# Keys of the first attention spread over the heads by 8 DMAs a tile instead of by multiplies with a mask, with the projected rows in another order

## The chip, the cores and the metric

One core of one Trainium2 chip runs the kernel. The metric is the device time in microseconds (us) from the first to the last instruction with what lies around them: 362.15 us, the median of 3 runs (362.09 to 362.67). The engines are TensorE (PE), VectorE (DVE), ScalarE (ACT), GpSimd (POOL) and SyncE (SP), which here only issues DMAs.

## The reference

Two layers work on x of shape (16, 64, 256), each an attention and a feed-forward block with a layernorm ahead and x added behind. The change touches the first attention only: 8 heads of 8 dimensions over 256 positions, for each of 16 batch entries.

```python
qkv = x @ w_in.T + b_in                      # x is the transposed, normalised input
scores = jnp.einsum('bqhd,bkhd->bhqk', q, k) / sqrt(8)
scores = jnp.where(band, scores, neg)        # |query - key| <= 64
attn = jax.nn.softmax(scores, axis=-1)
o = jnp.einsum('bhqk,bkhd->bqhd', attn, v)
y = relu(o @ w_out.T + b_out) * encodings
out = jnp.einsum('nit,io->not', y, w_ct) + b_ct
```

The feed-forward block of layer 0 picks the upper half of the tokens by a score and works on these; layer 1 has an attention of 32 heads and a squared-relu block with a mixture term.

## The kernel before

x stands in SBUF as 8 tiles of 128 rows; a tile holds two batch entries (b = 0, 1). The first attention runs as a software pipeline written by hand. Every engine walks the same list of slots `(T_, l)`, 16 slots a tile, and in each slot issues what its own `slot_` function says for it; the order within an engine is fixed by that code, and semaphores tie the engines together. `(T_, l)` works on unit `16 * T_ + l` of the scores, and on other steps with a lag.

A unit is one (b, g, c, w): batch entry, group of four heads, half of the queries, pair of heads. Its steps are

- the scores matmul into bank `S` (L339): the queries of a group are the weights, the keys of two heads the 384 moving columns;
- on DVE the band mask and the row maximum (L1110), two custom instructions for a unit;
- after 8 units four transposes of the maxima (L349), which ACT writes into rows 96 to 127 of `qp` (L791);
- 11 slots behind, two transposed score matmuls into `ST` (L361), then exp on ACT (L785), the band on POOL by four affine selects for two units (L978 to L985), and 16 slots behind the product with v (L377).

One matmul gives all heads of a group apart because the keys are spread: `kb` holds for each head j of a group a copy of the projected keys `kp` in which all rows but those of head j are zero. In rows 96 to 99 it holds a one for head j, which takes the maximum off. `kp` and `qp` carry each value in three rows (`r` = 0 to 2) as parts of a split into a rounded and a remaining piece. In the kernel before, row `32 r + 8 j + d` is part r of dimension d of head j, so the 24 rows of a head stand in three runs of 8.

The spread copies of a tile are written by

- POOL, three times 128x1024: `keys` (L953 to L961), `kp` times `kmask`, for (b, g) = (0,0), (0,1), (1,0), in the slots of the table `KB`;
- ACT, four times 128x256: L753 to L763, for (b, g) = (1,1), in the slots of `KA`.

They are made one tile ahead, in the slots `T_ = t - 1`: slots 3, 6, 9 and 12 (`PROJ`) project keys of group 0, keys of group 1, queries of group 0 and of group 1. ACT writes `hs`, the rounded piece, from the bank (L751), and DVE mixes it into `kp` or `qp` a slot later (L1208, semaphore `dve_mix`). `kb` is double buffered: for tile t the copy waits for `pe_st` of tile t - 2.

The start: ACT's queue loads `w0`, `b0`, `kmask` and `wv0`; DVE rounds `w0` to `w0h` (L1084), multiplies `b0` into `sb0` (L1086), normalises tile 0 (L1077) and takes the remainder `w0l` (L1094), which the first projection needs. SP's queue loads x and, behind it, all other weights.

The second half (layer 0's feed-forward, then layer 1) starts in the last slots of the pipeline and is not changed.

Of the kernel before, what the change touches and what calls it, by code (L numbers as in the profile page):

```python
# [47 lines left out]
def build(nc, a):  # L48
    ctx = ExitStack()
    with ctx:  # L50
# [93 lines left out]
        names = ("ld_first ld_w0 ld_small ld_x1 ld_x ld_rest ld_late st_out "  # L144
# [106 lines left out]
        def _(sp):  # L251
# [19 lines left out]
            late = [(b1[:, :], a["b1"]),  # L271
# [10 lines left out]
            assert len(late) == 12  # L282
# [7 lines left out]
        LATE = 16 * 12  # L290
# [3 lines left out]
        def _(pe):  # L294
            mm, tr = nc.tensor.matmul, nc.tensor.transpose

            def project(t, n):

                if n == 0:
                    pe.wait_ge(s["act_xh"], t + 1)  # L300
                    pe.wait_ge(s["dve_xl"], t + 1)
                    if t == 0:
                        pe.wait_ge(s["dve_w"], 4)
                bank = proj_bank(t, n)
                if t >= 1:
# [8 lines left out]
            def values(t):
                if t >= 1:
                    pe.wait_ge(s["dve_mix"], 4 * t + 4)
                if t == 0:
                    pe.wait_ge(s["ld_small"], 64)
# [181 lines left out]
            for T_, l in SLOTS_ALL:  # L500
# [3 lines left out]
                if T_ == 1 and l == 10:  # L504
                    pe.wait_ge(s["dve_w"], 5)
# [199 lines left out]
        def _(act):  # L705
# [5 lines left out]
            load(b0[:, :], a["b0"], "ld_w0")  # L711
            load(kmask[:, :], a["kmask"], "ld_small")
            load(wv0[:, :], a["wv0"], "ld_small")

            def slot_(T_, l):

                t = T_ - 2
                if 0 <= t < TILES:
# [23 lines left out]
                if 0 <= t < TILES:  # L742
                    if l - 1 in PROJ:
# [3 lines left out]
                        if m == 0:  # L747
                            act.wait_ge(s["dve_w"], 4)
                        if m >= 2:
                            act.wait_ge(s["dve_mix"], m - 1)  # L750
                        A(r32(hs[:, m % 2, :]), proj_bank(t, n)[:, :], ACT.Identity, bias=sb0[:, n:n + 1], scale=cols[:, n // 2:n // 2 + 1])\  # L751
                            .then_inc(s["act_hs"], 1)
                for t, j in ((T_ + 1, KA.get(l)), (T_, KA.get(l + UNITS))):  # L753
                    if j is not None and 0 <= t < TILES:
                        if j == 0:
                            act.wait_ge(s["dve_mix"], 4 * t + 2)
                            if t == 0:
                                act.wait_ge(s["ld_small"], 64)
                            if t >= 2:
                                act.wait_ge(s["pe_st"], UNITS * (t - 1))  # L760
                        last = A(r32(kb[:, t % 2, 1, j, 1, :]), kp[:, 1, 1, :], ACT.Copy, scale=kmask[:, j:j + 1])
# [174 lines left out]
        def _(pool):  # L936
# [16 lines left out]
            def keys(t, b, g):  # L953

                pool.wait_ge(s["dve_mix"], 4 * t + g + 1)
                if t == 0 and (b, g) == (0, 0):
                    pool.wait_ge(s["ld_small"], 64)
                if t >= 2:
                    pool.wait_ge(s["pe_st"], UNITS * (t - 2) + 8 * b + 4 * g + 4)
                G.tensor_tensor(r32(kb[:, t % 2, g, :, b, :]), kp[:, g, b:b + 1, :].to_broadcast([P, 4, T]),  # L960
                                kmask[:, :, None].to_broadcast([P, 4, T]), ALU.mult).then_inc(s["pool_kb"], 1)  # L961

            def slot_(T_, l):
# [24 lines left out]
                if l in KB and 0 <= t < TILES:  # L988
# [78 lines left out]
        def _(dve):  # L1067
# [22 lines left out]
            dve.wait_ge(s["dve_w"], 2)  # L1090
            dve.wait_ge(s["dve_zero"], 1)
            for b in range(2):
                hp = slice(64 * b, 64 * b + 64)
                V.tensor_tensor(r32(w0l[hp, b, :, :]), w0[hp, :, :], w0h[hp, :, :], ALU.subtract).then_inc(s["dve_w"], 1)  # L1094

            def slot_(T_, l):
# [96 lines left out]
                if (T_, l) == (-1, 2):  # L1193
                    dve.wait_ge(s["ld_small"], 64)
# [264 lines left out]
```

## Time and profile before

| | |
|---|---|
| runs | 362.09, 362.15, 362.67 us |
| profiled execution | 362.1 us, span 360.4 us |
| PE busy | 320.2 us (89% of the span) |
| DVE busy | 256.2 us (71%) |
| ACT busy | 208.1 us (58%) |
| POOL busy | 192.7 us (53%) |
| chain that ended last | PE 58%, DVE 27%, issue 8%, ACT 3% |

The span is from the first to the last instruction of the profiled execution; its own time has 1.7 us more. Busy shares over the whole span mix stages: DVE is near full in the first attention (to about 170 us) and far from it later. So the rows below are taken by stretch. A tile of the pipeline takes about 21 us of it.

### The profile page before, as it was taken

To read this page: it belongs to the slowest core of one execution; us is meant where nothing else is said; L and a number is where in the kernel's file an instruction comes from. 1 tells how busy PE (TensorE), PEld (TensorE's weight loads), DVE (VectorE), ACT (ScalarE), POOL (GpSimd) and SP (SyncE) were. 2 spreads that over 40 slices of the span, in tenths; PEclk is the share of its full clock that TensorE was granted. 3 is DMA by queue.
4 is the path that set the end of the run, shared out by engine and by line. 5 is a ranking of instruction groups with operands and counts; after the bars stand their busy time and mean duration, and the time that the engine had idled before them with its cause. 6 is when DMAs were issued, how large, how long until landed. Compare 5 with 4: busy or idle time off the path is not lost.

```text
span 360.4 us, 7398 instructions
## 1 busy us (share of the span) xinstructions
PE 320.2 (89%) x2258; PEld 252.3 (70%) x2258; DVE 256.2 (71%) x935; ACT 208.1 (58%) x438; POOL 192.7 (53%) x287
## 2 busy tenths in 40 slices
PE   0689999779798898999999999899999999999993
PEld 0467768567576666767777777777777767888892
DVE  5899999999989899988323615576478846661364
ACT  2639888759687695967841341467577865213210
POOL 4757988758767585856602431515152543244733
PEclk9859999999999999999999999999999999999997
DMA  7996000000000000000000000000000000000011
GB/s 220 363 373 227 1 3 3 1 2 3 1 2 0 3 3 1 3 2 2 2 2 0 0 2 0 1 2 0 2 3 0 2 0 3 0 31 15 1 38 37
DMA packets 10150, 12.16 MB, mean 34 GB/s; under 512 B 1920, under 2 KB 8832, under 8 KB 10112
## 3 DMA queue, kind: packets, MB, share of 16 engines
q1 hardware_dynamic: 9536, 11.36, 9.2%
q8 instruction: 20, 0.33, 0.4%
q10 hardware_dynamic: 576, 0.33, 0.4%
q14 instruction: 18, 0.15, 0.1%
HBM read 10.64 MB, written 1.05 MB: 32 GB/s over the span
## 4 chain that ended last, share of the span: by engine, by line
PE 58%; DVE 27%; issue 8%; ACT 3%; POOL 2%; DMA 1%; POOLq 0%; DVEq 0%; SPq 0%; ACTq 0%
DVE masked L1110 10%; PE S L666 6%; PE S L339 5%; PE O L377 4%; PE ST L690 4%; PE S L472 4%; PE ST L361 4%; PE S L608 2%; PE S L536 2%; PE PJ L449 2%; PE PJ L579 2%; PE O L623 2%; PE PJ L310 2%; DVE st L1072 2%; PE XB L597 2%
## 5 line engine op out<-in xcount | busy, mean ns | idle before, releaser
L1110 DVE CUSTOM_DVE_ANT_0 masked<-S,band 128x192 bf16<-128x192 f32 x256 | 79.1, 353 | 8.4 <-PE S L339 7.3
L785 ACT ACTIVATE ex<-ST 128x384 f32<-128x384 f32 x128 | 62.2, 489 | 14.0 <-PE ST L361 13.4
L339 PE MATMUL S<-qk 128*128 128x384 f32 x128 | 53.5, 424 | 10.2 <-DVE mw L1110 8.1
L948 POOL TENSOR_SCALAR rstd<-mv 128x1 f32<-128x1 f32 x40 | 11.8, 294 | 94.2 <-DVE mv L1074 94.0
L960 POOL TENSOR_TENSOR qk<-kp,kmask 128x1024 fp32r<-128x1024 f32 x24 | 46.3, 1934 | 5.0 <-DVE kp L1208 4.9
L361 PE MATMUL ST<-qk 128*128 128x192 f32 x256 | 48.7, 273 | 0.0
L361 PEld LDWEIGHTS ST<-qk 128*128 128x128 f32 x256 | 44.5, 189 | 1.9 <-issue 1.2
L339 PEld LDWEIGHTS S<-qk 128*128 128x128 f32 x128 | 24.8, 195 | 23.3 <-issue 16.1
L1254 DVE TENSOR_REDUCE mw<-S 128x8 f32<-128x512 f32 x32 | 22.0, 687 | 17.9 <-PE S L536 17.8
L751 ACT ACTIVATE hs<-PJ,sb,cols 128x512 fp32r<-128x512 f32 x29 | 22.5, 777 | 20.6 <-PE PJ L311 20.1
L377 PE MATMUL O<-ex,v 128*32 128x192 f32 x512 | 34.2, 338 | 0.0
L690 PE MATMUL ST<-down,hT 128*128 128x256 f32 x128 | 28.9, 379 | 0.0
L310 PE MATMUL PJ<-xs,w0h 128*128 128x256 f32 x58 | 18.6, 340 | 11.1 <-DVE xs L1191 10.0
L978 POOL TENSOR_SCALAR_AFFINE_SELECT ex<-ex 128x256 f32<-128x256 f32 x32 | 14.3, 448 | 24.4 <-ACT ex L785 24.3
L983 POOL TENSOR_SCALAR_AFFINE_SELECT ex<-ex 128x512 f32<-128x512 f32 x32 | 20.6, 642 | 12.2 <-ACT ex L785 12.2
L690 PEld LDWEIGHTS ST<-down,hT 128*128 128x128 f32 x128 | 23.8, 190 | 2.9
L951 POOL TENSOR_TENSOR rstd<-rstd,cols 128x1 f32<-128x1 f32 x40 | 22.7, 569 | 3.3
L666 PE MATMUL S<-qk 128*128 128x512 f32 x96 | 24.3, 402 | 0.0
L310 PEld LDWEIGHTS PJ<-xs,w0h 128*128 128x128 f32 x58 | 12.0, 206 | 15.8 <-issue 15.3
L895 ACT ACTIVATE ex<-ST 128x512 f32<-128x512 f32 x32 | 19.1, 597 | 5.3 <-PE ST L549 4.9
L1008 POOL TENSOR_TENSOR qk<-kp,kmask 128x512 fp32r<-128x512 f32 x16 | 16.5, 1056 | 9.9 <-DVE kp L1223 5.6
L1110 DVE DVE_READ_ACCUMULATOR2_ANT mw<- 128x1 f32 x256 | 21.2, 83 | 0.0
(178 smaller groups left out, 757.9 us busy)
## 6 DMA issues: line engine op xcount, KB each, us to landing
w<-in_w SPq DMA_DIRECT2D x2, 1024.0 KB, 10.1
cx<-in_cx SPq DMA_DIRECT2D x1, 1024.0 KB, 7.9
cxT<-in_cxT SPq DMA_DIRECT2D x1, 1024.0 KB, 9.6
up<-in_up SPq DMA_DIRECT2D x1, 1024.0 KB, 10.9
down<-in_down SPq DMA_DIRECT2D x1, 1024.0 KB, 11.8
out<-x SPq DMA_DIRECT2D x8, 128.0 KB, 1.7
x<-in_x SPq DMA_DIRECT2D x1, 768.0 KB, 5.6
vecs<-in_vecs SPq DMA_DIRECT2D x1, 640.0 KB, 8.0
```

Source lines behind the costliest of these rows:

```text
L310: mm(bank[:, T * b:T * b + T], r32(w0h[:, n, :]), r32(xs[:, b, :]), start=True, stop=False)
L339: mm(out, r32(qp[:, t % 2, g, b, P * c:P * c + P]), r32(mv_), start=True, stop=True).then_inc(s["pe_s"], 1)
L361: last = mm(ST[n % 2][:, WIN * h:WIN * h + WIN], r32(kb[:, t % 2, g, 2 * w + h, b, P * c:P * c + P]), r32(qp[:, t % 2, g, b, BAND * c:BAND ...
L377: last = mm(O[32 * j:32 * j + 32, T * g + BAND * c:T * g + BAND * c + WIN], v0[:, t % 2, c, b, 4 * g + j, :], ex[:, (n // 2) % 4, j, :], s ...
L666: last = mm(S[m % 2][:, :].rearrange("p (t c) -> p t c", t=4), r32(up2[:, a, k, P * f:P * f + P]), r32(xq[half][:, :, b, k, :]), start=(i ...
L690: last = mm(ST[t % 2][:, 0:T], hT[:, f, P * m:P * m + P], down[:, f, :], start=(f == 0), stop=(f == FC - 1))
L751: A(r32(hs[:, m % 2, :]), proj_bank(t, n)[:, :], ACT.Identity, bias=sb0[:, n:n + 1], scale=cols[:, n // 2:n // 2 + 1])\
L785: A(ex[:, (n // 2) % 4, 2 * w:2 * w + 2, :], ST[n % 2][:, 0:2 * WIN].rearrange("p (h k) -> p h k", h=2), ACT.Exp, scale=SCALE).then_inc(s[ ...
L951: G.tensor_tensor(rstd[:, t:t + 1], rstd[:, t:t + 1], cols[:, 2:3], ALU.pow).then_inc(s[done], 1)
L960: G.tensor_tensor(r32(kb[:, t % 2, g, :, b, :]), kp[:, g, b:b + 1, :].to_broadcast([P, 4, T]), kmask[:, :, None].to_broadcast([P, 4, T]), ...
L1110: last = V.tensor_tensor_reduce(out=masked[:, n % 2, h, :], in0=S[n % 2][:, WIN * h:WIN * h + WIN], in1=band[:, c, :], scale=1.0, scalar=N ...
L1254: V.tensor_reduce(mw[:, k % 2, 2 * g:2 * g + 2, 96:100], S[0][:, :].rearrange("p (i j k) -> p i j k", i=2, j=4), AX, ALU.max).then_inc(s[" ...
```

## The change

- The rows of a head become neighbours: row `24 j + 8 r + d` instead of `32 r + 8 j + d`. The host hands over the same arrays as before. The columns of `w0` are put in the new order on the chip, by a copy on ACT that writes `w0h` rounded (in place of DVE's L1084) and a copy on POOL into `w0p`, a free part of `hT`. `b0` is loaded in five DMAs instead of one. The masks by part and by head (`part0`, `kmask0`) are made by DVE from `ident`, which now is loaded ahead of the band; `kmask` goes to the end of SP's small loads.
- For tiles 0 and 1 POOL and ACT write `kb` as before, with `kmask0`.
- From tile 2 on 8 DMAs a tile on SP's queue copy the 24 rows of each head from `kp` to its block of `kb`: four (one for each head of a group, both groups in one DMA) for b = 0, four for b = 1. The zeros and the rows 96 to 127 of both buffers stay as tiles 0 and 1 left them. The first four wait for both key mixes of the tile and for `pe_st` of the first half of tile t - 2, the last four for `pe_st` of its second half. The scores wait for `ld_kb0` and `ld_kb1` instead of `pool_kb` and `act_kb`, and so does the next overwriting of `kp`.

```diff
+        w0p = hT[:, 4:8, 0:96]
+        KB_DMA = 16 * 4
@@ sync
             load(cols[:, :], a["cols"], "ld_first")
+            load(ident[:, :], a["ident"], "ld_ident")
             load(exf[:, 0:2 * WIN], a["band"], "ld_small")
-            load(ident[:, :], a["ident"], "ld_small")
...
-            late = [(b1[:, :], a["b1"]),
+            late = [(b1[:, :], a["b1"]), (kmask[:, :], a["kmask"]),
...
+            for t in range(2, TILES):
+                sp.wait_ge(s["dve_mix"], 4 * t + 2)
+                for b in range(2):
+                    sp.wait_ge(s["pe_st"], UNITS * (t - 2) + 8 * b + 8)
+                    for j in range(4):
+                        rows = slice(24 * j, 24 * j + 24)
+                        sp.dma_start(kb[rows, t % 2, :, j, b, :], kp[rows, :, b, :]).then_inc(s[f"ld_kb{b}"], 16)
@@ tensor
-                    if (b, g) == (1, 1):
+                    if t >= 2:
+                        pe.wait_ge(s[f"ld_kb{b}"], KB_DMA * (t - 1))
+                    elif (b, g) == (1, 1):
                         pe.wait_ge(s["act_kb"], t + 1)
@@ scalar
             load(w0[:, :, :], a["w0"], "ld_w0")
-            load(b0[:, :], a["b0"], "ld_w0")
-            load(kmask[:, :], a["kmask"], "ld_small")
+            for j in range(4):
+                load(b0[24 * j:24 * j + 24, :], a["b0"].rearrange("(r j d) n -> j r d n", r=4, j=4)[j, 0:3], "ld_b0")
+            load(b0[96:128, :], a["b0"][96:128, :], "ld_b0")
...
-                    if j is not None and 0 <= t < TILES:
+                    if j is not None and 0 <= t < 2:
...
+            act.wait_ge(s["ld_w0"], 16)
+            nc.scalar.copy(r32(w0h[:, :, 0:96]).rearrange("p n (j r d) -> p n j r d", j=4, r=3),
+                           w0[:, :, 0:96].rearrange("p n (r j d) -> p n j r d", r=3, j=4)).then_inc(s["act_w0"], 1)
@@ gpsimd
+            G.memset(w0h[:, :, 96:128], 0.0).then_inc(s["pool_w0"], 1)
+            pool.wait_ge(s["ld_w0"], 16)
+            G.tensor_copy(w0p.rearrange("p n (j r d) -> p n j r d", j=4, r=3),
+                          w0[:, :, 0:96].rearrange("p n (r j d) -> p n j r d", r=3, j=4)).then_inc(s["pool_w0"], 1)
...
-                if l in KB and 0 <= t < TILES:
+                if l in KB and 0 <= t < 2:
@@ vector
-            dve.wait_ge(s["ld_w0"], 32)
-            V.tensor_copy(r32(w0h[:, :, :]), w0[:, :, :]).then_inc(s["dve_w"], 1)
+            dve.wait_ge(s["ld_ident"], 16)
+            V.tensor_reduce(part0[:, :], ident[:, 0:96].rearrange("p (j r d) -> p r j d", j=4, r=3), mybir.AxisListType.XY, ALU.add)\
+                .then_inc(s["dve_part"], 1)
+            V.tensor_reduce(kmask0[:, :], ident[:, 0:96].rearrange("p (j k) -> p j k", j=4), AX, ALU.add).then_inc(s["dve_part"], 1)
+            dve.wait_ge(s["dve_part"], 2)
+            V.tensor_tensor(kmask0[:, :], kmask0[:, :], ident[:, 96:100], ALU.add).then_inc(s["dve_part"], 1)
+            dve.wait_ge(s["ld_b0"], 16 * 5)
...
-                V.tensor_tensor(r32(w0l[hp, b, :, :]), w0[hp, :, :], w0h[hp, :, :], ALU.subtract).then_inc(s["dve_w"], 1)
+                V.tensor_tensor(r32(w0l[hp, b, :, 0:96]), w0p[hp, :, :], w0h[hp, :, 0:96], ALU.subtract).then_inc(s["dve_w"], 1)
...
-                    if n < 2 and t >= 1:
+                    if n < 2 and t in (1, 2):
                         dve.wait_ge(s["pool_kb"], 3 * t)
...
+                    if n < 2 and t >= 3:
+                        dve.wait_ge(s["ld_kb0"], KB_DMA * (t - 2))
+                        dve.wait_ge(s["ld_kb1"], KB_DMA * (t - 2))
```

On POOL, in the slots of a tile of the steady part (rstd is the layernorm's, ex the exponentials, qk the array that holds `kb` and `qp`), this stood before:

```order
L948 TENSOR_SCALAR rstd<-mv 128x1
L951 TENSOR_TENSOR rstd<-rstd,cols 128x1
L978 AFFINE_SELECT ex<-ex 128x4x64
L980 AFFINE_SELECT ex<-ex 128x4x128
L960 TENSOR_TENSOR qk<-kp,kmask 128x4x256
L983 AFFINE_SELECT ex<-ex 128x4x128
L985 AFFINE_SELECT ex<-ex 128x4x64
```

And this stands there now:

```order
L967 TENSOR_SCALAR rstd<-mv 128x1
L970 TENSOR_TENSOR rstd<-rstd,cols 128x1
L995 AFFINE_SELECT ex<-ex 128x4x64
L997 AFFINE_SELECT ex<-ex 128x4x128
L1000 AFFINE_SELECT ex<-ex 128x4x128
L1002 AFFINE_SELECT ex<-ex 128x4x64
```

The multiply is gone from between the selects, in three places of each tile from tile 2 on.

On SP, behind the loads (gw and ew are weights of the last block), this stood before:

```order
L253 DMA up<-in_up 128x2x1024
L253 DMA down<-in_down 128x8x256
L253 DMA eg<-in_ew 128x2x256
L253 DMA eg<-in_gw 128x2x8
L288 DMA out<-x 128x256 [waits h_out] x8
```

And this stands there now, for the first of six tiles:

```order
L257 DMA down<-in_down 128x8x256
L257 DMA eg<-in_ew 128x2x256
L257 DMA eg<-in_gw 128x2x8
L295 DMA qk<-kp 24x2x256 [waits pe_st,dve_mix]
L295 DMA qk<-kp 24x2x256 x3
L295 DMA qk<-kp 24x2x256 [waits pe_st]
L295 DMA qk<-kp 24x2x256 x3
```

Eight DMAs a tile come in behind the last load and ahead of the stores.

On DVE, at the start of the program (sb is the bias `sb0`, xn the normalised tile 0), this stood before:

```order
L1074 BN_AGGR mv<-st 128x2 [waits dve_ln]
L1084 CAST w0h<-w 128x512 [waits ld_w0]
L1086 TENSOR_TENSOR sb<-b,cols 128x1 x4
L1077 TENSOR_SCALAR xn<-x,mv,rstd 128x256 [waits pool_rstd]
L1094 TENSOR_TENSOR w0l<-w,w0h 64x512 [waits dve_zero,dve_w]
L1094 TENSOR_TENSOR w0l<-w,w0h 64x512
L1190 TENSOR_TENSOR xs<-xn,xs 64x256 [waits act_xh]
```

And this stands there now:

```order
L1091 BN_AGGR mv<-st 128x2 [waits dve_ln]
L1101 TENSOR_REDUCE part<-ident 128x3 [waits ld_ident]
L1103 TENSOR_REDUCE kmask<-ident 128x4
L1105 TENSOR_TENSOR kmask<-kmask,ident 128x4 [waits dve_part]
L1108 TENSOR_TENSOR sb<-b,part 128x1 [waits ld_b0]
L1108 TENSOR_TENSOR sb<-b,part 128x1 x3
L1094 TENSOR_SCALAR xn<-x,mv,rstd 128x256 [waits pool_rstd]
L1117 TENSOR_TENSOR w0l<-hT,w0h 64x4x96 [waits pool_w0,act_w0,dve_zero]
L1117 TENSOR_TENSOR w0l<-hT,w0h 64x4x96
L1213 TENSOR_TENSOR xs<-xn,xs 64x256 [waits act_xh]
```

The cast of the weights has left DVE, three short instructions have come in, the bias waits for the five pieces of `b0`, and the remainder waits for ACT and POOL.

## Rows read from the trace of the kernel before

**Rows 1.** The page, part 2: busy tenths and PE's clock in 40 slices.
```profile
DVE  5899999999989899988323615576478846661364
PEclk9859999999999999999999999999999999999997
```

**Rows 2.** Stretches, one per tile: start:end, length, busy us (instructions), clock, DMA share.
```profile
110.00:131.40 21.40, 18.35 (x161) 14.00 (x161) 20.05 (x89) 15.84 (x35) 15.36 (x24) 1.00 0.01 2
...
47.00:68.00 21.00, 19.61 (x184) 15.27 (x176) 19.67 (x89) 18.45 (x41) 18.60 (x26) 1.00 0.01 2
sum 121.50, PE 106.93 PEld 81.59 DVE 113.15 ACT 91.05 POOL 87.64; mean PE 17.82 PEld 13.60 DVE 18.86 ACT 15.18 POOL 14.61
```

**Rows 3.** Groups by line and shape, 31 to 165 us, of POOL and of ACT.
```profile
L960 POOL TENSOR_TENSOR qk<-kp,kmask 128x1024 fp32r<-128x1024 f32 x19 | 36.9, 1942 | 1.7 <-DVE kp L1208 1.6
L761 ACT ACTIVATE qk<-kp,kmask 128x256 fp32r<-128x256 f32 x26 | 13.2, 509 | 0.3
```

**Rows 4.** DVE and POOL in order of time: start, length, instruction.
```profile
66.06 2.33 POOL L960 TENSOR_TENSOR qk<-kp,kmask 128x1024 fp32r<-128x1024 f32 x1
66.67 1.86 DVE L1151 TENSOR_SCALAR hT<-x,mv,rstd 128x256 f32<-128x256 f32 x1
88.82 1.97 POOL L960 TENSOR_TENSOR qk<-kp,kmask 128x1024 fp32r<-128x1024 f32 x1
89.58 1.50 DVE L1156 CUSTOM_DVE_ANT_0 cmp<-hT,vecs 128x256 f32<-128x256 f32 x1
96.80 1.89 POOL L960 TENSOR_TENSOR qk<-kp,kmask 128x1024 fp32r<-128x1024 f32 x1 [0.45 <-DVE kp L1208]
97.84 0.93 DVE L1169 TENSOR_SCALAR sel<-slot,rk 128x128 f32<-128x128 f32 x1
```

**Rows 5.** The same DVE lines later, without a multiply beside them.
```profile
172.70 0.35 DVE L1169 TENSOR_SCALAR sel<-slot,rk 128x128 f32<-128x128 f32 x1
180.99 0.42 DVE L1156 CUSTOM_DVE_ANT_0 cmp<-hT,vecs 128x256 f32<-128x256 f32 x1
196.73 0.40 DVE L1151 TENSOR_SCALAR hT<-x,mv,rstd 128x256 f32<-128x256 f32 x1
```

**Rows 6.** A DVE instruction beside one of POOL's selects.
```profile
92.28 0.63 POOL L983 TENSOR_SCALAR_AFFINE_SELECT ex<-ex 128x512 f32<-128x512 f32 x1 [0.34 <-ACT ex L785]
92.35 0.84 DVE L1191 TENSOR_TENSOR xs<-xn,xs 64x256 fp32r<-64x256 f32 x1
```

**Rows 7.** Waits of PE, 47 to 169.4 us: total, times, longest.
```profile
PE S L339 <- DVE mw L1110: 5.5, 13, 1.5
PE MT L415 <- DVE sel L1169: 4.3, 4, 1.3
```

**Rows 8.** Second key mix of a tile, and that tile's first scores matmul.
```profile
79.64 0.75 DVE L1208 SCALAR_TENSOR_TENSOR kp<-PJ,b,hs 128x512 fp32r<-128x512 f32 x1
88.56 0.42 PE L339 MATMUL S<-qk 128*128 128x384 f32 x1
```

**Rows 9.** DMA issues of the whole run: KB each, median us to landing.
```profile
out<-x SPq DMA_DIRECT2D x8, 128.0 KB, 1.7
b<-in_b ACTq DMA_DIRECT2D x1, 2.0 KB, 3.4
down<-in_down SPq DMA_DIRECT2D x1, 1024.0 KB, 11.8
```

**Rows 10.** The start, in order of time.
```profile
1.22 0.45 ACTq L709 DMA_DIRECT2D b<-in_b  x1
5.31 0.36 DVE L1086 TENSOR_TENSOR sb<-b,cols 128x1 f32<-128x1 f32 x4
6.18 0.41 DVE L1077 TENSOR_SCALAR xn<-x,mv,rstd 128x256 f32<-128x256 f32 x1 [0.51 <-POOL rstd L951]
6.51 1.40 DVE L1094 TENSOR_TENSOR w0l<-w,w0h 64x512 fp32r<-64x512 f32 x2
...
8.89 0.55 PE L310 MATMUL PJ<-xs,w0h 128*128 128x256 f32 x1 [8.89 <-DVE xs L1191]
```

More of the change, by code:

```diff
@@ L68, in build @@
         cols = sb("cols", [P, 4])
+        part0 = sb("part0", [P, 3])
+        kmask0 = sb("kmask0", [P, 4])
         tri = sb("tri", [P, P])
@@ L141, in build @@
         XB = pb("XB", [P, 512])
-        names = ("ld_first ld_w0 ld_small ld_x1 ld_x ld_rest ld_late st_out "
+        names = ("ld_first ld_w0 ld_b0 ld_ident act_w0 pool_w0 dve_part ld_small ld_x1 ld_x ld_rest ld_late st_out "
                  "pe_proj pe_v pe_s pe_mt pe_st pe_pv pe_ot pe_bt pe_out pe_wct pe_bias "
@@ L281, in _ @@
                     (eg[:, :, T:T + NEXP], a["gw"].rearrange("(k p) f -> p k f", p=P))]
-            assert len(late) == 12
+            assert len(late) == 13
             for dst, src in late:
                 load(dst, src, "ld_late")
+            for t in range(2, TILES):
[5 more added lines that the diff above has]
+                        sp.dma_start(kb[rows, t % 2, :, j, b, :], kp[rows, :, b, :]).then_inc(s[f"ld_kb{b}"], 16)
             ov = a["out"].rearrange("(t p) c -> p t c", p=P)
@@ L289, in _ @@
             sp.wait_ge(s["st_out"], 16 * TILES)
-        LATE = 16 * 12
+        LATE = 16 * 13
         @block.tensor
@@ L302, in project @@
                     if t == 0:
-                        pe.wait_ge(s["dve_w"], 4)
+                        pe.wait_ge(s["dve_w"], 3)
                 bank = proj_bank(t, n)
@@ L317, in values @@
                 if t == 0:
-                    pe.wait_ge(s["ld_small"], 64)
+                    pe.wait_ge(s["ld_small"], 32)
                 pe.wait_ge(s["dve_xn"], t + 1)
@@ L504, in _ @@
                 if T_ == 1 and l == 10:
-                    pe.wait_ge(s["dve_w"], 5)
+                    pe.wait_ge(s["dve_w"], 4)
                 slot_(T_, l)
@@ L724, in slot_ @@
                         if t == 0:
-                            act.wait_ge(s["dve_w"], 5)
+                            act.wait_ge(s["dve_w"], 4)
                         if t >= 1:
@@ L747, in slot_ @@
                         if m == 0:
-                            act.wait_ge(s["dve_w"], 4)
+                            act.wait_ge(s["dve_w"], 1)
                         if m >= 2:
                             act.wait_ge(s["dve_mix"], m - 1)
-                        A(r32(hs[:, m % 2, :]), proj_bank(t, n)[:, :], ACT.Identity, bias=sb0[:, n:n + 1], scale=cols[:, n // 2:n // 2 + 1])\
+                        A(r32(hs[:, m % 2, :]), proj_bank(t, n)[:, :], ACT.Identity, bias=sb0[:, n:n + 1], scale=part0[:, 1 + n // 2:2 + n // 2])\
                             .then_inc(s["act_hs"], 1)
                 for t, j in ((T_ + 1, KA.get(l)), (T_, KA.get(l + UNITS))):
-                    if j is not None and 0 <= t < TILES:
+                    if j is not None and 0 <= t < 2:
                         if j == 0:
@@ L757, in slot_ @@
                             if t == 0:
[L758 to L761, printed above, removed]
+                                act.wait_ge(s["dve_part"], 3)
+                        last = A(r32(kb[:, t % 2, 1, j, 1, :]), kp[:, 1, 1, :], ACT.Copy, scale=kmask0[:, j:j + 1])
                         if j == 3:
@@ L956, in keys @@
                 if t == 0 and (b, g) == (0, 0):
-                    pool.wait_ge(s["ld_small"], 64)
-                if t >= 2:
-                    pool.wait_ge(s["pe_st"], UNITS * (t - 2) + 8 * b + 4 * g + 4)
+                    pool.wait_ge(s["dve_part"], 3)
                 G.tensor_tensor(r32(kb[:, t % 2, g, :, b, :]), kp[:, g, b:b + 1, :].to_broadcast([P, 4, T]),
-                                kmask[:, :, None].to_broadcast([P, 4, T]), ALU.mult).then_inc(s["pool_kb"], 1)
+                                kmask0[:, :, None].to_broadcast([P, 4, T]), ALU.mult).then_inc(s["pool_kb"], 1)
             def slot_(T_, l):
@@ L1081, in _ @@
             stats(0, x[:, 0, :], "dve_ln", 0)
-            dve.wait_ge(s["ld_w0"], 32)
-            V.tensor_copy(r32(w0h[:, :, :]), w0[:, :, :]).then_inc(s["dve_w"], 1)
+            dve.wait_ge(s["ld_ident"], 16)
[5 more added lines that the diff above has]
+            dve.wait_ge(s["ld_b0"], 16 * 5)
             for n in range(4):
-                last = V.tensor_tensor(sb0[:, n:n + 1], b0[:, n:n + 1], cols[:, n // 2:n // 2 + 1], ALU.mult)
+                last = V.tensor_tensor(sb0[:, n:n + 1], b0[:, n:n + 1], part0[:, 1 + n // 2:2 + n // 2], ALU.mult)
             last.then_inc(s["dve_w"], 1)
@@ L1193, in slot_ @@
                 if (T_, l) == (-1, 2):
-                    dve.wait_ge(s["ld_small"], 64)
+                    dve.wait_ge(s["ld_small"], 32)
                     V.tensor_copy(band[:, :, :], exf[:, 0:2 * WIN].rearrange("p (c k) -> p c k", c=2)).then_inc(s["dve_band"], 1)
```

5 lines of the change are left out of this document (3 added, 2 removed).

## The prediction

> **What bounds the kernel now.** I read the page by slices first, then the engines in stretches of one tile, then DVE and POOL against the clock in order of time, then the waits of PE, and last the DMAs and the start.
>
> In the slices DVE is at nine tenths from the fifth to the eighteenth, which is the first attention to about 170 us, and PE's clock is full there [rows 1]. By stretches of a tile, the six in which tile 2 is under way to the last (47 to 169.4 us, 121.5 us together) hold 113.15 us of DVE and 106.93 us of PE [rows 2]: 93% and 88%, with POOL at 72% and ACT at 75%. So DVE sets the pace and PE is close behind it. The reader is to see that neither POOL nor ACT is the bound. What is taken from them counts only by what it does to DVE and PE.
>
> It does something to DVE. At 66.06 us POOL starts the multiply L960, 2.33 us long, and DVE's L1151, started at 66.67, takes 1.86 us. It ends at 68.53, just behind the multiply at 68.39 [rows 4]. With nothing of that kind beside it the same instruction takes 0.40 us [rows 5]. L1156 takes 1.50 against 0.42, L1169 0.93 against 0.35 [rows 4, 5], each until the multiply beside it is over (90.79 and 98.69 us). DVE runs these in order with its row maxima, so PE gets its next bank later: PE waits 5.5 us for L1110 and 4.3 us for L1169 in the six stretches [rows 7].
>
> **The change part by part.**
>
> *The multiplies.* 18 of L960's 24 and 24 of L761's 32 go: 18 x 1.942 = 35 us of POOL and 24 x 0.509 = 12.2 us of ACT [rows 3]. As work on engines at three quarters I price both at nothing; lighter queues on both can only bring exp and the selects forward, which I leave to the range.
>
> *DVE's stalls.* Beside the 18 multiplies stand ten long DVE instructions: two L1151, stalled by 1.45 and 1.33 us, three L1156 by 1.08, 1.06 and 1.06, four L1169 by 0.58, 0.58, 0.58 and 0.60, and one L1190 by 0.60. One of each of the first three kinds is in [rows 4] and its undisturbed length in [rows 5]; the L1190 took 1.02 instead of 0.42. The sum is 8.9 us. They all go. What stays are stalls beside the selects, as 0.84 instead of 0.42 at L1191 while L983 ran [rows 6]; some 5 us of these over the attention, and the ten can now meet a select instead of nothing. POOL without the multiplies is busy (87.64 - 35) / 121.5 = 0.43 of the time [rows 2, 3]; ten meetings at that chance and 0.3 us each return about 1 us, so the stall that goes is 8 to 9 us.
>
> The page SBUF — State Buffer of the Trainium skill (section Who interferes with whom) says that DVE with two SBUF inputs, or in a two-port mode, and GpSimd shut each other out for whole instructions, and that the order of issue decides. The ends of the stalls agree with it. It also speaks against a full gain here: the selects read SBUF as the multiply does and keep that lock. By that rule the stalls turn into shorter ones, which is the 1 us above.
>
> *What of it the end sees.* DVE would fall from 113.15 to 104.2 us in the six stretches, and PE, at 106.93, would be the fuller engine [rows 2]. The fullest that PE gets in a stretch of this stage is 19.61 of 21.00 us, 93.4% [rows 2]. At that share its 106.93 us need 114.5 us, 7.0 less than 121.5. With DVE the limit at its own fullest share, 20.05 of 21.40 or 93.7%, it would be 111.2 us, 10.3 less. The least is what PE waits for directly behind a stalled instruction, the four L1169: 2.3 us. The ends are thus 2.3 and 10.3; I take 7.0, less half a microsecond for the new meetings with selects: 6.5.
>
> *The DMAs.* 48 on SP, of 24 rows x 2 KB = 48 KB each, in groups of four. Before, SP waits for nothing but the stores at that time, so nothing is queued behind their waits; the stores come 100 us later. For b = 0 the wait ends with the second key mix, at 79.64 + 0.75 = 80.39 us for tile 4, and the first scores matmul of that tile starts at 88.56 us [rows 8]: 8.2 us. An issue takes about 0.45 us [rows 10], so the fourth starts 1.4 us on, and 6.8 us are left to land. A store of 128 KB lands in 1.7 us, a 1 MB load among others in 11.8 [rows 9]. DMA is at 0.01 of its capacity in these stretches [rows 2], so the store is the nearest row, and 1.7 to 3.4 us my figure. Both groups then land some microseconds ahead of need, and I price them at nothing. The second group waits for `pe_st` of tile t - 2 three slots later (some 4 us) and is needed eight slots later than the first. The next overwriting of `kp`, at slot 4 of the next tile, comes later than either. If the cover were gone each microsecond of lateness would cost six, one for each tile.
>
> The page DMA: Bandwidth & Descriptors (section Why a DMA increments its semaphore by 16 and not by 1) says that a copy is cut over the largest number of engines up to 16 that divides both outer sizes. By it 24 rows go over 12 engines and the parts of `b0`, with an outer size of 3, over 3. That would make 4 KB for each of the 12, less than the 8 KB that 16 would carry of the store's 128 KB, so by the rule too the sum stays. No row of before shows such a split.
>
> *The start.* `b0` came with an issue at 1.22 us that landed in 3.4 [rows 9, 10]. Now it is five issues on ACT's queue, the fifth at 1.22 + 4 x 0.47 = 3.10 us; with 3.4 it lands at 6.5 us. The four `sb` take 0.36, xn 0.41 [rows 10]: xn ends at 7.3 instead of 6.6. Behind it L1094, 0.70 us for 64x512, has 384 columns of 512 left, in proportion 0.53, so the two take 1.05 instead of 1.40 [rows 10], end at 8.4 instead of 7.9, and PE starts 0.5 us later than 8.89. ACT's table load moves behind seven issues, to 4.1 us, and its copy of `w0` ends near 6.2; POOL's copy of 384 elements, between a select's 0.63 for 512 [rows 6] and half of a multiply, ends near 5.1. Both are done before 7.3. I take +0.5. Below, the cast of 0.39 us saved on DVE could make it 0; above, pieces of `b0` that each need twice the issue time land 1.9 us later, for +2.4. This part stands ahead of all else and passes through whole.
>
> *The sum.* -6.5 + 0.5 = -6.0. The profiled execution took 362.1 us, as good as the median of 362.15; 362.1 - 6.0 = 356.1.
>
> **The rivals.**
>
> *DVE stays the limit and PE shrinks with it.* PE's busy time holds matmuls that were stretched behind waits, so 106.93 may not be its need. Then the 10.3 us count: 362.1 - 10.3 + 0.5 = 352.3. For it speaks that DVE is the fuller engine in five of the six stretches, against it that PE, DVE and ACT hand two banks around, so that a stretch fills neither.
>
> *PE covers the stalls anyway.* PE has transposed scores and products with v queued while DVE stalls, and only the stall before L415 is waited for at once [rows 7]. Then 2.3 us count, and the time is 362.1 - 2.3 + 0.5 = 360.3. Against it: a DVE at 93% cannot make up for a lost microsecond later.
>
> *Slower: the DMAs land late.* The place is the first scores matmul of each tile, L339. It decides from 6.8 us of landing on, and eats up the 6.0 us at 7.8. At the 11.8 us of the loads it would be 6 x 5.0 = 30 us, at 8.5 us of landing 6 x 1.7 = 10.2, so 366. Against it: idle queues, and landing times of 1.7 us.
>
> *The change doesn't do what it says.* The multiplies are gone from POOL's and ACT's order for tiles 2 to 7, so this could only be that stalls move whole from the multiply to the selects: 0 + 0.5, 362.6.
>
> **How the numbers follow.** The forecast of 356.1 has 0.52, with a range of its own of 354 to 358.5. The greater gain (352.3) has 0.16, the covered stalls (360.3) 0.17, the late DMAs 0.08, the stalls that only move 0.07. The range of 352.0 to 360.8 leaves out the last two and the outer parts of the second and third. A measurement of this kernel can tell 0.2%, 0.7 us, from no change. Faster holds the first three: 0.85. Of the last 0.07 some 0.04 is no change; the remainder with the late DMAs is slower, 0.11.
>
> **What would show it.** In the profile after: L1151, L1156 and L1169 of the tiles in the attention near 0.41, 0.42 and 0.35 us, or 0.3 more beside a select; the stretches of a tile near 20 instead of 21.4 us, PE above 90% in them; kb's DMAs landed in 1.7 to 3.4 us and no wait of L339 for a DMA; PE's first matmul at 9.3 to 9.5 us instead of 8.89. It would be wrong if PE's wait for L1110 grows by what L1169 loses, if the stalls come back beside the selects, if L339 waits for the queue, or if the first matmul is later than 10 us.

## The result and the profile after

| | before | after |
|---|---|---|
| median of 4 runs | 362.12 us (362.02 to 362.67) | 356.35 us (355.79 to 356.77) |
| profiled execution: time, span | 362.1, 360.4 us | 356.8, 355.0 us |
| DVE busy | 256.2 us | 245.8 us |
| POOL busy | 192.7 us | 159.2 us |
| ACT busy | 208.1 us | 200.6 us |

The ratio is 0.9837, with a 95% interval of 0.9819 to 0.9854: 5.8 us faster. The forecast was 356.1 us. The total is right; two of its terms are not, and they cancel.

The page of the kernel after, part 2, for the lines of [rows 1]:

```profile
DVE  2699999998989898977324534575578746761364
PEclk9999999999999999999999999999999999999999
```

DVE now starts late, with a 2 and a 6 in the first two slices, and its nines are mixed with eights. The start of the kernel after, in order of time, for [rows 10] (ACTq and SPq are the issuing of DMAs on the queues of ACT and of SP):

```profile
1.23 4.04 ACTq L722 DMA_DIRECT2D b<-in_b  x5
5.77 1.28 ACT L838 ACT_TABLE_LOAD   x1 [5.77 <-issue]
7.17 0.49 ACT L841 CAST w0h<-w 128x384 fp32r<-128x384 f32 x1
10.57 0.37 DVE L1108 TENSOR_TENSOR sb<-b,part 128x1 f32<-128x1 f32 x4 [4.62 <-DMA b<-in_b]
13.29 0.55 PE L321 MATMUL PJ<-xs,w0h 128*128 128x256 f32 x1 [13.29 <-DVE xs L1214]
```

DVE waits 4.62 us for `b0`, and PE's first matmul is at 13.29 us instead of 8.89: 4.4 us lost. The five issues took 4.04 us. The chain of waits of the kernel after shows the first four, and the last from its issue at 4.83 us to its landing:

```profile
1.23 1.33 ACTq L722
...
2.59 0.71 ACTq L722
3.33 0.71 ACTq L722
4.07 0.72 ACTq L722
...
4.83 5.72 DMA b<-in_b
```

The stretches of a tile of the kernel after (columns as in [rows 2]; the first, the fourth and the last, and the sum of all six):

```profile
51.80:71.00 19.20, 18.43 (x169) 14.72 (x166) 17.68 (x89) 16.10 (x34) 10.93 (x22) 1.00 0.11 27
...
109.80:129.00 19.20, 17.92 (x162) 14.05 (x162) 18.04 (x93) 14.79 (x32) 9.83 (x21) 1.00 0.10 24
...
147.70:163.60 15.90, 15.56 (x144) 11.93 (x143) 13.70 (x84) 10.98 (x25) 8.11 (x18) 1.00 0.01 2
sum 111.80, PE 105.11 PEld 81.87 DVE 103.04 ACT 84.20 POOL 57.70; mean PE 17.52 PEld 13.64 DVE 17.17 ACT 14.03 POOL 9.62
```

The one from 109.8 us takes 19.2 us, where the one from 110 us before took 21.4, the six together 111.8 instead of 121.5, and DVE's busy time in them fell by 113.15 - 103.04 = 10.1 us. The same DVE instructions as in [rows 4], groups by line and shape of the kernel after from 34 to 165 us (line, operation, count, busy, mean ns). Line numbers shift from kernel to kernel: L1151 (hT), L1156 (cmp) and L1169 (sel) of the kernel before are L1174, L1179 and L1192 here, and in what follows the names of the arrays tell which is meant.

```profile
L1179 DVE CUSTOM_DVE_ANT_0 cmp<-hT,vecs 128x256 f32<-128x256 f32 x6 | 2.9, 489 | 0.0
L1174 DVE TENSOR_SCALAR hT<-x,mv,rstd 128x256 f32<-128x256 f32 x6 | 2.5, 411 | 0.0
...
L1192 DVE TENSOR_SCALAR sel<-slot,rk 128x128 f32<-128x128 f32 x5 | 1.7, 345 | 0.2
```

They are at their undisturbed lengths of [rows 5], L1179 but for two meetings with a select.

To part start and tiles: tile 2's values are computed at 47.16 us before and 51.79 after, and tile 5 is normalised for the feed-forward block (L1151, now L1174), the last such step inside the attention, at 169.10 us before and 163.82 after. Between the two the kernel before took 121.9 us and the kernel after 112.0. The tiles gave 9.9 us, the start took 4.4 to 4.6, and nothing much changed behind: 360.4 - 355.0 = 5.4 us of span.

### The profile page after: what moved, and what is told of

Same layout as the page of the kernel before. It is cut to its first block, busy times and chain, and to the rows that moved or that the text cites. A ratio compares the mean times of both kernels' runs of the same rounds, so it can differ in the third digit from the quotient of the medians.

```text
span 355.0 us, 7395 instructions
## 1 busy us (share of the span) xinstructions
PE 319.8 (90%) x2258; PEld 253.6 (71%) x2258; DVE 245.8 (69%) x937; ACT 200.6 (57%) x415; POOL 159.2 (45%) x271
## 4 chain that ended last, share of the span: by engine, by line
PE 63%; DVE 21%; issue 6%; ACT 3%; POOL 2%; DMA 2%; ACTq 1%; SPq 0%; POOLq 0%; DVEq 0%
DVE masked L1133 8%; PE S L679 6%; PE S L352 6%; PE O L390 5%; PE ST L374 4%; PE ST L703 4%; PE S L485 4%; PE PJ L321 2%; PE S L621 2%; PE S L549 2%; PE PJ L462 2%; PE PJ L592 2%; PE O L636 2%; PE XB L610 2%; PE MT L647 2%
## 5 line engine op out<-in xcount | busy, mean ns | idle before, releaser
L352 PEld LDWEIGHTS S<-qk 128*128 128x128 f32 x128 | 25.4, 200 | 17.8 <-issue 10.2
L765 ACT ACTIVATE hs<-PJ,sb,part 128x512 fp32r<-128x512 f32 x29 | 22.5, 778 | 17.4 <-PE PJ L322 17.0
L679 PEld LDWEIGHTS S<-qk 128*128 128x128 f32 x96 | 17.7, 188 | 4.3 <-issue 0.4
```

The lines of the kernel that those rows point to most:

```text
L352: mm(out, r32(qp[:, t % 2, g, b, P * c:P * c + P]), r32(mv_), start=True, stop=True).then_inc(s["pe_s"], 1)
L679: last = mm(S[m % 2][:, :].rearrange("p (t c) -> p t c", t=4), r32(up2[:, a, k, P * f:P * f + P]), r32(xq[half][:, :, b, k, :]), start=(i ...
```

## Experiments: start and tiles

**b0 in one DMA.** The host's array has its rows in the new order; all else is the kernel after.

```diff
-            for j in range(4):
-                load(b0[24 * j:24 * j + 24, :], a["b0"].rearrange("(r j d) n -> j r d n", r=4, j=4)[j, 0:3], "ld_b0")
-            load(b0[96:128, :], a["b0"][96:128, :], "ld_b0")
+            load(b0[:, :], a["b0"], "ld_b0")
...
-    arr["b0"] = b0.reshape(P, 4)
+    arr["b0"] = b0.reshape(P, 4)[order]
```

> The changed kernel with one edit: b0 is handed over with its rows already in the new order and loaded by one DMA instead of five. Theory (the start is held by the pieces of b0): in the changed kernel DVE waits 4.6 us for b0 and PE's first matmul is at 13.29 us, 4.4 later than before. With one DMA b0 lands near 4.7 us, ACT's queue is free at 2.6 instead of 5.7, and PE starts at 9.2 to 9.6 us: 356.35 - 3.9 = 352.4 us, 352.0 to 353.0. Rival A (the copies of w0 on ACT and POOL hold the start as well): PE starts at 11 us or later, 354 to 356. Rival B (the pipeline behind makes up a late start): PE starts near 9.4 and the time stays within 0.7 us of 356.35.

Measured: 351.69 us, ratio to before 0.9707 (0.9691 to 0.9724). Its start, in order of time:

```profile
1.22 0.45 ACTq L722 DMA_DIRECT2D b<-in_b  x1
...
4.17 0.51 ACT L839 CAST w0h<-w 128x384 fp32r<-128x384 f32 x1 [0.48 <-DMA w<-in_w]
...
6.08 0.41 DVE L1092 TENSOR_SCALAR xn<-x,mv,rstd 128x256 f32<-128x256 f32 x1 [0.33 <-POOL rstd L968]
6.41 1.13 DVE L1115 TENSOR_TENSOR w0l<-hT,w0h 64x384 fp32r<-64x384 f32 x2
...
8.53 0.55 PE L321 MATMUL PJ<-xs,w0h 128*128 128x256 f32 x1 [8.53 <-DVE xs L1212]
```

One DMA takes back all of the start and 0.4 us more, so start and time both lie below the theory's ranges (9.2 to 9.6 and 352.0 to 353.0 us). The two remainders, 384 wide instead of 512, take 1.13 us instead of 1.40 [rows 10], and xn starts 0.10 us earlier. The cast that has left DVE gives nothing here, since xn waits for POOL's rstd in both kernels. The time fell by 4.7 us for 4.8 us of start. Both rivals fall: the copies of `w0` hold nothing, and nothing makes up a late start.

**b0 in four wide DMAs.** From the kernel with one DMA:

```diff
-            load(b0[:, :], a["b0"], "ld_b0")
+            for n in range(4):
+                load(b0[:, n:n + 1], a["b0"][n], "ld_b0")
```

> As b0_one, but b0 comes in four DMAs, one for each of its four columns and each over all 128 rows. It tells the number of DMAs apart from their form: in the changed kernel the four pieces of 24 rows take 1.33, 0.71, 0.71 and 0.72 us to issue, the piece of 32 rows 0.44. Theory (the form counts: an outer size of 3 uses few DMA engines and costs 0.7 us an issue; 128 rows cost 0.45): the last column is issued at 2.6 us and lands near 6.5, PE starts at 9.3 to 9.8 us, 352.3 to 353.2 us. Rival (each DMA beyond the first costs what the pieces cost): last issue near 4.3 us, landing near 9, PE starts near 12 us, 354.7 to 355.7.

Measured: 353.27 us, ratio 0.9751 (0.9737 to 0.9765). In order of time:

```profile
1.22 1.90 ACTq L722 DMA_DIRECT2D b<-in_b  x4
...
7.24 0.37 DVE L1107 TENSOR_TENSOR sb<-b,part 128x1 f32<-128x1 f32 x4 [1.79 <-DMA b<-in_b]
...
9.96 0.55 PE L321 MATMUL PJ<-xs,w0h 128*128 128x256 f32 x1 [9.96 <-DVE xs L1213]
```

Four issues over 128 rows take 1.90 us, five of which four have an outer size of 3 take 4.04. Start and time are 0.2 and 0.1 us beyond the range of the theory and far from the rival's. So of the 4.7 us that `b0` costs, 353.27 - 351.69 = 1.6 is the price of more DMAs, and 356.35 - 353.27 = 3.1 that of their narrow form (and of a fifth). Reckoned against the kernel before run beside each, it is 1.8 and 3.2. The later issues also land later: 5.72 us against 3.4 [rows 9]. SP's loads of x were issued meanwhile; that they are the cause isn't shown.

**Rows handed over in the new order, start as before.** The kernel before, with the DMAs of keys and their waits, the masks as extra columns of `kmask` and `cols`, and

```diff
-    arr["w0"] = w0.reshape(P, 4, P)
-    arr["b0"] = b0.reshape(P, 4)
+    arr["w0"] = w0.reshape(P, 4, P)[:, :, order]
+    arr["b0"] = b0.reshape(P, 4)[order]
```

> The kernel before with the DMAs of keys from tile 2 on, and with w0, b0 and the two masks handed over in the new order (loaded as before, DVE rounds w0 as before): no work of the new start is left. Theory (start +4.4 us, tiles -10.2 us, and the two add): first matmul at 8.9 us and 362.1 - 10.2 = 351.9 us, 351.3 to 352.6. Rival A (the tiles gain so much because they start late, when the big loads are over): 354 to 356. Rival B (the start costs more than the first matmul shows): under 351.

Measured: 352.52 us, ratio 0.973 (0.9715 to 0.9744), in the theory's range; the first matmul at 8.73 us. Against the 362.52 us of the kernel before run beside it that is 10.0 us faster with nearly the same start, and it is what the DMAs of keys are worth.

**The new start alone.** The kernel after without its DMAs of keys:

```diff
-                    if j is not None and 0 <= t < 2:
+                    if j is not None and 0 <= t < TILES:
...
-                if l in KB and 0 <= t < 2:
+                if l in KB and 0 <= t < TILES:
```

> The changed kernel without its DMAs of keys: POOL and ACT spread the keys of all eight tiles as before, the rows are in the new order and the start is the new one. Theory (the two parts add): 362.1 + 4.4 = 366.5 us, 366.0 to 367.2, with L1174, L1179 and L1192 of DVE stalled as before (1.7, 1.5 and 0.93 us). Rival (part of the 4.4 us is made up later whatever the keys do): 363 to 365.

Measured: 366.02 us, ratio 1.0104 (1.0089 to 1.0119), within the theory's range at its lower edge; the first matmul at 12.88 us. DVE's groups from 40 to 165 us:

```profile
L1174 DVE CUSTOM_DVE_ANT_0 cmp<-hT,vecs 128x256 f32<-128x256 f32 x5 | 5.8, 1159 | 0.0
L1169 DVE TENSOR_SCALAR hT<-x,mv,rstd 128x256 f32<-128x256 f32 x5 | 4.8, 964 | 0.0
L1187 DVE TENSOR_SCALAR sel<-slot,rk 128x128 f32<-128x128 f32 x5 | 4.1, 819 | 0.2
```

The stalls are back. The start itself is 0.4 us shorter here than in the kernel after (12.88 against 13.29). The parts add: 366.02 with the start, 352.52 with the DMAs, 356.35 with both, and 362.5 + 3.5 - 10.0 = 356.0 by the two differences from the kernel before run beside them.

## Experiments: what the tiles gained from

**ACT's copies back.** The DMAs carry only what POOL's multiplies carried:

```diff
+                        gs = slice(0, 2 - b)
-                        sp.dma_start(kb[rows, t % 2, :, j, b, :], kp[rows, :, b, :]).then_inc(s[f"ld_kb{b}"], 16)
+                        sp.dma_start(kb[rows, t % 2, gs, j, b, :], kp[rows, gs, b, :]).then_inc(s[f"ld_kb{b}"], 16)
...
-                    if j is not None and 0 <= t < 2:
+                    if j is not None and 0 <= t < TILES:
```

> The changed kernel with the four copies of keys a tile back on ACT ((b, g) = (1, 1)); the DMAs carry only what POOL's multiplies carried. Theory (the gain is the end of DVE's stalls behind POOL's multiplies; ACT at three quarters of its time has room): 356.35 to 356.9 us. Rival (ACT's 12.2 us are the share of the gain, 10.2 against 6.5, that I had not forecast): 358 to 360 us, with ACT's exp later and waits of PE for it.

Measured: 356.22 us, ratio 0.9836 (0.9812 to 0.9861), no different from the kernel after. ACT carried its copies again (the group from 31 to 165 us):

```profile
L776 ACT ACTIVATE qk<-kp,kmask 128x256 fp32r<-128x256 f32 x27 | 13.7, 509 | 0.3
```

12 us of ACT are worth nothing here.

**Multiplies for nothing.** The kernel after, with a multiply of the same size in each slot in which one had stood, its result used by nobody:

```diff
+                if l in KB and 2 <= t < TILES:
+                    b, g = KB[l]
+                    pool.wait_ge(s["dve_mix"], 4 * t + g + 1)
+                    pool.wait_ge(s["ld_rest"], 64)
+                    pool.wait_ge(s["pool_idle"], 3 * (t - 2) + g + 2 * b)
+                    G.tensor_tensor(r32(idle[:, :, :]), cx[:, 0:1, :].to_broadcast([P, 4, T]),
+                                    kmask0[:, :, None].to_broadcast([P, 4, T]), ALU.mult).then_inc(s["pool_idle"], 1)
```

> The changed kernel with three multiplies of 128x1024 a tile added on POOL for tiles 2 to 7, in the same slots and behind the same waits as the kernel before had them, but from cx into an unused part of hT: nothing waits for them. Theory (what the change took away is DVE's stalls while POOL reads and writes SBUF): DVE's L1175, L1181 and L1193 (hT, cmp, sel) are stalled again and the time goes back by most of the 10 us: 364 to 367 us. Rival (the gain came from PE and DVE no longer waiting for POOL's results, or from kp being free earlier): 356.35 to 358 us.

Measured: 366.82 us, ratio 1.0119 (1.0098 to 1.014). DVE and POOL of this kernel in order of time:

```profile
93.22 1.97 POOL L1013 TENSOR_TENSOR hT<-cx,kmask 128x1024 fp32r<-128x1024 f32 x1
93.99 1.49 DVE L1187 CUSTOM_DVE_ANT_0 cmp<-hT,vecs 128x256 f32<-128x256 f32 x1
101.35 1.89 POOL L1013 TENSOR_TENSOR hT<-cx,kmask 128x1024 fp32r<-128x1024 f32 x1 [0.45 <-DVE kp L1242]
102.39 0.93 DVE L1200 TENSOR_SCALAR sel<-slot,rk 128x128 f32<-128x128 f32 x1
```

10.5 us come back, all that the tiles had gained, though no one waits for the results. It was the presence of the multiplies, not the wait for what they made.

**Memsets for nothing.** Two memsets of 128x1024 in place of each such multiply:

```diff
-                    G.tensor_tensor(r32(idle[:, :, :]), cx[:, 0:1, :].to_broadcast([P, 4, T]),
-                                    kmask0[:, :, None].to_broadcast([P, 4, T]), ALU.mult).then_inc(s["pool_idle"], 1)
+                    for i in range(2):
+                        pool.wait_ge(s["pool_idle"], 2 * (3 * (t - 2) + g + 2 * b) + i)
+                        G.memset(idle[:, :, :], 0.0).then_inc(s["pool_idle"], 1)
```

> The same with two memsets of 128x1024 (0.97 us each, 1.94 together) in place of each multiply: POOL is as busy, and writes SBUF but reads nothing. By the Trainium skill's SBUF — State Buffer (section Who interferes with whom) a DVE instruction with two SBUF inputs contends only with a GpSimd instruction that reads, one in a two-port mode with both. If so the custom L1179 (cmp from hT and vecs) keeps its 0.42 us and the tensor_scalar forms L1174 and L1192 (hT, sel) are stalled by up to 1 us: 358 to 362 us. Theory without that rule (any work of POOL stalls DVE): as with multiplies, 364 to 367. Rival (POOL's reads alone matter): 356.35 to 357.5.

Measured: 362.81 us, ratio to before 1.0012 (0.9996 to 1.0028), 6.5 us over the kernel after. In order of time:

```profile
91.81 1.99 POOL L1013 MEMSET hT<- 128x1024 f32 x2
91.96 0.95 DVE L1181 TENSOR_SCALAR hT<-x,mv,rstd 128x256 f32<-128x256 f32 x1
93.38 0.41 DVE L1186 CUSTOM_DVE_ANT_0 cmp<-hT,vecs 128x256 f32<-128x256 f32 x1
99.06 1.96 POOL L1013 MEMSET hT<- 128x1024 f32 x2 [0.29 <-DVE kp L1241]
100.13 0.97 DVE L1199 TENSOR_SCALAR sel<-slot,rk 128x128 f32<-128x128 f32 x1
```

The custom instruction with two SBUF inputs runs at its 0.41 us beside a memset, where it took 1.49 beside a multiply. The tensor_scalar forms are stalled by either. By the Trainium skill, SBUF — State Buffer (section Who interferes with whom), a DVE instruction with two SBUF inputs contends only with a GpSimd instruction that reads SBUF, and one in a two-port mode, which tensor_scalar can enter, with any. The trace agrees for all three. The time is 0.8 us above what I had given that case. One more tensor_scalar was hit than I had counted, the normalising of the next tile, whose mean was 0.47 us in the kernel before (the group from 31 to 175 us):

```profile
L1101 DVE TENSOR_SCALAR xn<-x,mv,rstd 128x256 f32<-128x256 f32 x5 | 6.9, 1370 | 0.0
```

**Multiplies moved.** The kernel before, with one line changed:

```diff
-        KB = {5: (0, 0), 9: (0, 1), 14: (1, 0)}
+        KB = {7: (0, 0), 9: (0, 1), 11: (1, 0)}
```

> The kernel before with one line changed: POOL's three multiplies of a tile in slots 7, 9 and 11 instead of 5, 9 and 14, away from the slots in which DVE has L1151 (15), L1156 (0) and L1169 (5). All of the work stays. Theory (the loss lies in the meetings of these instructions with the multiplies, not in POOL's load): the three are at 0.41, 0.42 to 0.66 and 0.35 to 0.64 us, and the time is 353 to 357 us. Rival (what counts is that selects stand behind multiplies, so exp results reach PE late): 360 us or more, since three multiplies in a row hold the selects longer than before.

Measured: 354.79 us, ratio 0.9787 (0.9771 to 0.9804). In order of time:

```profile
95.28 0.34 DVE L1169 TENSOR_SCALAR sel<-slot,rk 128x128 f32<-128x128 f32 x1
97.02 1.89 POOL L960 TENSOR_TENSOR qk<-kp,kmask 128x1024 fp32r<-128x1024 f32 x1
100.37 1.93 POOL L960 TENSOR_TENSOR qk<-kp,kmask 128x1024 fp32r<-128x1024 f32 x1
103.23 1.89 POOL L960 TENSOR_TENSOR qk<-kp,kmask 128x1024 fp32r<-128x1024 f32 x1
106.95 0.70 DVE L1151 TENSOR_SCALAR hT<-x,mv,rstd 128x256 f32<-128x256 f32 x1
108.13 0.59 DVE L1156 CUSTOM_DVE_ANT_0 cmp<-hT,vecs 128x256 f32<-128x256 f32 x1
```

All 35 us of multiplies are still there, and 7.8 us are gone, more than the whole change gave. What stays, 0.70 and 0.59 instead of 0.41 and 0.42, are meetings with selects. In the profiled executions 0.5 us of the gain lies ahead of tile 2, whose values are at 46.65 us instead of 47.16; from there to the normalising of tile 5 it is 121.9 - 115.2 = 6.7 us, where the change gave 9.9. So the meetings are most of the cost, and POOL's load and what else the multiplies do have at most some 3 us, which no run divides.

## Experiments: the DMAs' cover, and the best version

**DMAs held back.**

```diff
-                sp.wait_ge(s["dve_mix"], 4 * t + 2)
+                sp.wait_ge(s["dve_mix"], 4 * t + 4)
```

> The changed kernel with the eight DMAs of a tile held back until the last query mix (slot 13 instead of 8, near 89.8 instead of 82.6 us for tile 4, whose first scores matmul is at 90.8). It shows when the DMAs land, which the trace doesn't give. Theory (issues of 0.78 us, the fourth 2.3 us behind the first, landing some 2.1 us behind its issue): the first group lands at 94.2 us instead of 87.0, 3.4 us late, the second in time for slot 8; six tiles make +18 to +22 us less what DVE and PE make up: 370 to 378 us. Rival (in the changed kernel the landing is already at the edge, which the waits of L352 put down to DMA speak for): the whole shift of 7.2 us counts, 6 x 7.2 = 43 us, 395 to 400 us.

Measured: 388.37 us, ratio 1.0709 (1.068 to 1.0738), between the ranges of theory and rival. For tile 4, in order of time:

```profile
97.73 6.53 SPq L295 DMA_DIRECT2D qk<-kp  x8
...
102.37 0.44 PE L352 MATMUL S<-qk 128*128 128x384 f32 x1 [3.46 <-DMA qk<-kp]
```

The first group has landed at most 102.37 - 97.73 = 4.6 us after its first issue. In the kernel after the first issue is at 82.63 us and the matmul at 90.77: 3.5 us to spare. This kernel's PE waited 21.9 us in six such places. What the other 10 us of its 32 are is not shown. PE's granted clock is 0.87 to 0.93 in the stretches from 103 to 200 us, where the kernel after has 1.00, and the steps that lag behind the scores may run empty and fill again; how the 10 us divide was not tried.

It also shows how to read a wait of the kernel after. Its waits of PE and of the weight loads in the stretch from 51.8 to 163.6 us:

```profile
PE S L352 <- DMA qk<-kp: 0.3, 1, 0.3
...
PEld S L352 <- DMA qk<-kp: 3.9, 10, 0.5
```

These look like late keys, as the rival in the expectation took them. But the one matmul is

```profile
146.47 0.41 PE L352 MATMUL S<-qk 128*128 128x384 f32 x1 [0.34 <-DMA qk<-kp]
...
108.50 0.41 PE L352 MATMUL S<-qk 128*128 128x384 f32 x1 [0.33 <-DVE mw L1133]
```

the same slot of another tile, with the same wait put down to DVE. Both are matmuls of the tile at work, whose keys landed a tile ago; the DMA that came last by the profile is one of the next tile on the same semaphore. The ten waits of the weight loads are five pairs of 0.30 and 0.48 us at these slots of five tiles. The last tile, behind which no DMAs come, has the same pair without them:

```profile
161.83 0.19 PEld L352 LDWEIGHTS S<-qk 128*128 128x128 f32 x1 [0.30 <-issue]
162.78 0.19 PEld L352 LDWEIGHTS S<-qk 128*128 128x128 f32 x1 [0.48 <-issue]
```

So has the kernel before (0.30 and 0.47 at 86.12 and 87.06 us). A real wait for these DMAs is 3.46 us long.

**One DMA for b0 and moved multiplies.** From the kernel with one DMA, the same line of `KB` as above, which now holds for tiles 0 and 1 only.

> b0_one with POOL's multiplies, left for tiles 0 and 1 alone, in slots 7, 9 and 11 instead of 5, 9 and 14: the two changes that gained, together. The multiplies of tile 1 meet L1190 and others of DVE up to 1.1 us; in mult_moved tile 2 began 0.5 us earlier than before. Theory: 351.0 to 351.5 us against 351.69. Rival (start-up of tile 0 waits for its first multiply, which a later slot can only delay): 351.7 to 352.5.

Measured: 350.99 us, ratio 0.9698 (0.9675 to 0.9721), the fastest here. Five of its six executions took 350.69 to 351.14 us; the profiled one took 353.83, with a mean granted clock of 0.953. Tile 2's values start at 45.90 us instead of 46.69. The interval overlaps that of `b0` in one DMA alone, and against the kernel before run beside each the gain is 0.4 us and not 0.7, so it is likely but not shown.

## Why the prediction was right, and where it was not

- *What bounds the kernel:* right. DVE set the pace, and its stalls beside POOL's multiplies were the loss. The multiplies for nothing and the moved ones show it from both sides.
- *The multiplies, as load on POOL and ACT:* nothing for ACT, as said: 356.22 us with its copies back against 356.35. For POOL the moved multiplies leave some 3 us at most, in which it is not told from the meetings that stayed.
- *DVE's stalls:* 8.9 us forecast, less 1 us for new meetings with selects. DVE's busy time fell by 10.1 us. The new meetings hardly came, and some of the old ones with selects went as well: the mean of L1191 of before fell from 0.69 to 0.51 us. Two slips of reading change nothing: three of the fourteen slices called nine tenths show an 8 [rows 1], and ten meetings at 0.43 and 0.3 us are 1.3 us, not 1.
- *What of it the end sees:* mis-sized. I took 6.5 us and gave 10.3 as the upper end and as a rival of its own. It was 10.0 by the kernel with the start of before, 10.5 by the multiplies for nothing and 9.9 between two places of the traces. The step that failed is "the fullest that PE gets in a stretch is 93.4%" with PE's busy time kept at 106.93 us. PE went to 105.11 of 111.80 us, 94.0%, with less busy time, and to 15.56 of 15.90 us in the last stretch. Of the 3.2 us that the six stretches gave beyond the forecast, the smaller busy time is 2.0 at the share of 93.4%, the higher share 0.7, and the meetings that did not come 0.5. The same 943 matmuls stand between the two places of the traces before and after, and their recorded lengths in sum are the same (159.8 and 159.6 us); they lie closer over one another, and so their busy time is less. A busy time of pipelined matmuls is no floor, and a share that was the fullest under one bound is no ceiling under another. The rival of the greater gain, which had 0.16, has the size that the tiles gave. Its mechanism holds in half: PE's busy time shrank, but by less than DVE's, so that PE (94.0%) and not DVE (92.2%) is the fuller engine afterwards.
- *The DMAs:* priced at nothing, and they cost nothing that a trace shows. An issue takes 0.78 us and not 0.45, though: the fourth ends 3.1 us behind the start of the first and starts 2.4 behind it, and 2.2 are left for landing. The 4.6 us in all lie in the 3.1 to 4.8 that the forecast's terms make, and of the 8.2 us of cover 3.5 were to spare.
- *The start:* mis-sized, +0.5 forecast, +4.4 measured, outside the 2.4 that I had as its upper end. I had the chain (five issues, the landing, the bias, the normalising) but took issue and landing from one DMA of 128 rows, issued at 1.22 us: 0.45 and 3.4 us. The pieces of 24 rows took 0.71 to 1.33 us to issue, so the last was issued at 4.83 us and not 3.10, and it landed in 5.72: 1.7 us late by the issues and 2.3 by the landing. The page DMA: Bandwidth & Descriptors of the Trainium skill (section Why a DMA increments its semaphore by 16 and not by 1), which I used only for the bytes of an engine, says in the same place that the issuing sequencer itself writes the increments of the engines that a copy doesn't use. The dearer issues here are those with an outer size that is no multiple of 16 (0.71 us for 3 and 0.78 for 24, against 0.44 for 32 and 0.45 for 128), which agrees with it in kind. That this is the cause isn't shown: the pieces of `b0` also have one more dimension, the DMAs of keys are on SP's queue, and two of SP's loads of 128 rows (band and bcol) took 0.63 and 0.64 us to issue here but 0.43 each in the kernel with one DMA for `b0`.
- The sum: -6.5 + 0.5 forecast, about -10 + 4.4 measured. That the total came out within 0.3 us is luck.

## What to carry to other kernels

Before moving work off an engine with room, look at which instructions of the full engine run long beside it: lines whose longest case was 2.7 to 4.6 times their shortest were meetings here, and moving the other engine's work by two or three slots gave most of what removing it gives (7.8 of 10.0 us, for one line). Price a small DMA at the head of a kernel by its place in the queue and by the form of its rows, and give constants to the kernel in the order in which it needs them. A forecast has to be read term by term: this one was right by two errors of 4 us.

## What was not expected of the hardware

- Issue of a DMA: 0.44 to 0.45 us on ACT's queue for pieces of 32 and 128 rows, 0.71 us with an outer size of 3, 0.78 us on SP's queue with 24 rows. The first of the narrow ones on ACT's queue took 1.33 us. The form of a DMA is not all: two of SP's loads of 128 rows took 0.63 and 0.64 us to issue while ACT issued its narrow pieces, and 0.43 each where ACT issued one DMA for `b0`.
- The landing of a small load grew from 3.4 us (issued at 1.22 us) to 5.7 (issued at 4.83), while SP had issued other loads.
- A memset on POOL stalls DVE's tensor_scalar (0.95 us instead of 0.41) but not a custom instruction with two inputs in SBUF (0.41).
- A gap of 3.5 us in PE's work in each tile went with a granted clock of 0.87 to 0.93 in the stretches that followed, where the kernel after had 1.00. The mean clock was 0.940 to 0.949 in all four executions of the kernel with the gaps and 0.981 to 0.999 in the four of the kernel after. A kernel without such gaps had 0.953 in one execution of six, so gaps are not the only thing that goes with less.
